# Last feed-forward layer's second product as three products of split parts, with the activations split by GpSimd and the weights split between key tiles

## What is computed

```python
def _L1_xattn_ref(q, k, mask, Wq, bq, Wk, bk, Wv, bv, Wo, bo):
    qh = einsum('bld,dh->blh', q, Wq) + bq
    kh = einsum('bld,dh->blh', k, Wk) + bk
    vh = einsum('blh,hv->blv', kh, Wv) + bv
    scores = where(mask == 0, -10000, einsum('bqh,bkh->bqk', qh, kh))
    return einsum('blh,hv->blv', softmax(scores) @ vh, Wo) + bo

def _L1_ffn_ref(x, W1, b1, phases, w_real, w_imag, W2, b2):   # D_FF = 1024
    hidden = einsum('bsd,df->bsf', x, W1) + b1
    imag = w_imag * sin(phases + hidden * 0.1)
    qphase = cos(phases) * w_real + sin(phases) * w_imag
    act = relu(hidden + qphase * imag * 0.1)
    return einsum('bsf,fd->bsd', act, W2) + b2

x = _layernorm(x + _L1_xattn_ref(x, ctx, mask, ...))
x = _layernorm(x + _L1_ffn_ref(x, ...))
```

## Time and profile before

| | |
|---|---|
| time, median of 3 runs | 3661.45 us (3659.2 to 3665.86) |
| the profiled execution | 3662.63 us, its span 3660.8 us |
| mean granted TensorE clock | 0.976 |
| busy share of the span | PE 93%, PEld 70%, DVE 72%, ACT 61%, POOL 28% |
| phase 3, main part | from 3079 us to the end |

### The profile page before, as it was taken

One profiled execution on the slowest core, in us unless ns is written; L12 is line 12 of the kernel. 1 busy time (PEld: TensorE's weight loads), 2 busy tenths in 40 slices (PEclk: granted clock), 3 DMA queues, 4 the chain that ended last, 5 costly groups with the idle time before them and its releaser, 6 DMA issues.

```text
span 3660.8 us, 61512 instructions
## 1 busy us (share of the span) xinstructions
PE 3401.6 (93%) x21474; PEld 2561.6 (70%) x21474; DVE 2627.9 (72%) x7168; ACT 2226.4 (61%) x4067; POOL 1008.0 (28%) x1560
## 2 busy tenths in 40 slices
PE   4999999999999948999999999999999876999998
PEld 3677777777777636777777777777777655766664
DVE  5588888888888754667777776777777643788876
ACT  3577767776777632455555555555555643677776
POOL 1144434444444431222222222222222210000000
PEclk8999999999999979999999999999999987999999
DMA  6554445545564221444444444444444421011010
GB/s 190 88 92 90 79 83 102 107 75 87 94 104 79 33 87 31 77 82 92 87 86 92 92 89 93 87 90 93 91 87 84 76 38 75 12 35 35 24 35 23
DMA packets 203410, 283.39 MB, mean 77 GB/s; under 512 B 48929, under 2 KB 131874, under 8 KB 194274
## 3 DMA queue, kind: packets, MB, share of 16 engines
q1 hardware_dynamic: 203106, 279.46, 39.0%
HBM read 179.49 MB, written 96.73 MB: 75 GB/s over the span
## 4 chain that ended last, share of the span: by engine, by line
PE 78%; DMA 6%; DVE 6%; ACT 4%; issue 3%; POOL 2%; SPq 1%; PEld 0%; POOLq 0%; PEldq 0%; ACTq 0%; DVEq 0%
PE ps L827 36%; PE ps L1001 10%; PE ps L975 9%; PE ps L1015 7%; PE ps L1199 5%; DMA k_stack<-qk_scratch 5%; PE ps L950 2%; PE ps L979 2%; PE ps L1075 1%; ACT pt L1677 1%; POOL pt L1877 1%; PE ps L1026 1%; PE ps L989 1%; SPq L2002 1%; PE ps L885 1%
## 5 line engine op out<-in xcount | busy, mean ns | idle before, releaser
L1677 ACT ACTIVATE pt<-ps 128x512 f32<-128x512 f32 x1280 | 723.3, 597 | 272.1 <-PE ps L1001 225.6
L1877 POOL TENSOR_SCALAR_AFFINE_SELECT pt<-pt 128x256 f32<-128x256 f32 x1024 | 389.2, 416 | 897.9 <-ACT pt L1677 897.8
L975 PE MATMUL ps<-k_stack,q_stack 96*128 96x512 f32 (+3 forms) x2048 | 587.8, 347 | 34.2 <-DMA k_stack<-qk_scratch 21.9
L1356 DVE CUSTOM_DVE_ANT_0 ps<-ps,future 128x512 f32<-128x512 f32 (+3 forms) x1024 | 482.3, 515 | 101.0 <-PE ps L975 94.7
L1001 PE MATMUL ps<-q_stack,k_stack 100*128 100x512 f32 (+3 forms) x2048 | 532.2, 342 | 14.7 <-ACT pt L1677 10.3
L975 PEld LDWEIGHTS ps<-k_stack,q_stack 96*128 96x128 f32 x2048 | 385.0, 194 | 118.4 <-DMA k_stack<-qk_scratch 26.6
L1349 DVE TENSOR_REDUCE nmax<-ps 128x1 f32<-128x512 f32 (+2 forms) x768 | 359.8, 505 | 120.4 <-PE ps L979 117.2
L1001 PEld LDWEIGHTS ps<-q_stack,k_stack 100*128 100x128 f32 x2048 | 344.8, 192 | 86.9 <-ACT pt L1677 35.5
L1883 POOL TENSOR_TENSOR rs<-rs,mhalf 128x4 f32<-128x4 f32 x96 | 97.1, 1011 | 1057.6 <-DVE rs L1392 1056.2
L1015 PE MATMUL ps<-pt,v_ones 128*32 128x512 f32 (+3 forms) x4096 | 304.9, 438 | 8.0 <-POOL pt L1877 8.0
L1661 ACT ACTIVATE q_stack<-ps 4x512 fp32r<-4x512 f32 x512 | 260.9, 573 | 54.3 <-PE ps L989 51.7
(11 more groups left out here) (276 smaller groups left out, 7969.9 us busy)
## 6 DMA issues: line engine op xcount, KB each, us to landing
qk_scratch<-parts SPq DMA_DIRECT2D x64, 1024.0 KB, 5.7
q_stack<-qk_scratch SPq DMA_DIRECT2D x384, 128.0 KB, 6.2
k_stack<-qk_scratch SPq DMA_DIRECT2D x384, 128.0 KB, 6.7
gate_of<-gate_scratch SPq DMA_DIRECT2D x128, 256.0 KB, 6.3
x_mid<-x_ring SPq DMA_DIRECT2D x32, 512.0 KB, 4.0
x_ring<-x_mid SPq DMA_DIRECT2D x32, 512.0 KB, 5.0
x_ring<-in_x SPq DMA_DIRECT2D x16, 512.0 KB, 3.9
out_dram<-x_ring SPq DMA_DIRECT2D x16, 512.0 KB, 2.9
```

Source lines behind the costliest of these rows:

```text
L975: done = e.matmul(bank(bank_of[piece])[:, at:at + width], a.q[0:96, base + h, t * P:(t + 1) * P], a.k[0:96, base + h, 0:width], start=True ...
L1356: done = e.tensor_tensor_reduce(src, src, future[:, SEQ - width:SEQ], -1.0, 3e38, ALU.add, ALU.min, nmax[:, g % 2, u // 5 * 2 + h, t:t + 1])
L1677: e.activation(dst, src, ACT.Exp).then_inc(exp_up.sem)
L1877: done = e.affine_select(out=blk, in_=blk, compare_op=ALU.is_ge, fill=0.0, base=0, pattern=[[0, 2], [1, P]], channel_multiplier=-1)
```

## The change

- `fd` becomes three fp32r products for each half of the outputs (six matmuls of 512 columns instead of two float32 ones), with the weights `wf2` as high and low parts in phase 3's weight buffer.
- GpSimd gets a piece `fc`: act_h = copy of act in fp32r, then act_l = act - act_h, both 128 x 512. It waits for ACT's `fc` of this block and for PE's `fd` of block i-3. PE's `fd` waits for GpSimd; ACT's `fc` waits for GpSimd's split of block i-3 instead of PE's `fd` of i-3.
- Phase 3's weights are six chunks. Two are split ahead of the key tiles, as they must be, and chunks 2 to 5 behind key tiles 1, 3, 5 and 7; the PE's warming matmuls start after one chunk instead of two. The separate load of w_down is gone.
- The table of phase 3 is new. Orders of one period, from `fa` 0 of item b on (' is item b-1):
  - PE before: fa0 cs fd6' fd7' fa1 fa2 bk' cp fa3 tm cw fd0 fa4 fd1 fa5 fd2 fa6 fd3 fa7 fd4 tc-x1 fd5 tc-ff
  - PE after: fa0 fd5' fd6' fd7' fa1 bk' fa2 cp fa3 tm fd0 fa4 cw fa5 fd1 fa6 fd2 fa7 fd3 tc-x1 fd4 tc-ff cs
  - DVE before: fa0 ce fb0 fa1 ln-ff' fb1 fa2 lm-ff' fa3 fb2 ln-x1 fb3 fa4 lm-x1 fb4 fa5 fb5 fa6 fa7 fb6 fb7 tc-x1 cw tc-ff cs
  - DVE after: fa0 ce fb0 fa1 ln-ff' fb1 fa2 lm-ff' fa3 fb2 ln-x1 fb3 fa4 lm-x1 cw fa5 fb4 fb5 fa6 fa7 fb6 tc-x1 fb7 cs tc-ff
  - ACT after: fa0 ce fb0 bk' fa1 fc0 fa2 fb1 cp fa3 fc1 fb2 lm-ff' fc2 fb3 fa4 cw fa5 fc3 fb4 lm-x1 fc4 fb5 fa6 fa7 fc5 fb6 tc-x1 fc6 fb7 fc7 tc-ff
  - POOL after: fc0 ln-ff' fc1 fc2 ln-x1 fc3 to fc7
- In phase 1's prologue `ab` and `trig` are loaded ahead of x, four[0] of each head moves from DVE to ACT, and the copy into the query stack from ACT to GpSimd, behind its constants.

```diff
-    dict(xqT=CT * 256, xk=CT * 256, xv=CT * 256, xo=CT * 256, w1=CT * FF),
+    dict(xqT=CT * 256, xk=CT * 256, xv=CT * 256, xo=CT * 256, w1=CT * FF, w2=FT * DIM),
...
-    3: (31.45, {
+    3: (32.91, {
...
+        act_h, act_l = (sb(st3, f"act_{part}", [P, DEEP, SEQ], F32R) for part in "hl")
...
-        wf1 = W3.get("w1", CT)
+        wf1, wf2 = W3.get("w1", CT), W3.get("w2", FT)
...
-        W3_READY = n
+        W3_READY = n - len(W3.chunks) + 2
...
-                    e.wait_ge(w_lo.sem, W3_READY - 2)
+                    e.wait_ge(w_lo.sem, W3_READY - 1)
...
                 elif kind == "fd":
                     b, i = key
-                    e.wait_ge(*fc_up[key])
+                    e.wait_ge(*fc_parts[key])
...
                     for c in range(CT):
-                        done = e.matmul(bank(6 + c), wf2[:, i, c * P:(c + 1) * P], act[:, i % DEEP, :], start=i == 0,
-                                        stop=i == FT - 1)
+                        cols = slice(c * P, (c + 1) * P)
+                        done = product(e, bank(6 + c), three(wf2[0][:, i, cols], wf2[1][:, i, cols],
+                                                             act_h[:, i % DEEP, :], act_l[:, i % DEEP, :]),
+                                       start=i == 0, stop=i == FT - 1)
...
-                                e.tensor_scalar(four[:, i, 0, :], trig[:, 0, :], ab[:, 0, h:h + 1], None,
-                                                ALU.mult).then_inc(mine.up())
-                                e.wait_ge(*mine.now)
+                                if h >= 2:
+                                    e.wait_ge(q_lo, h - 1)
+                                e.wait_ge(q_part, h + 1)
...
-                    for w, at, cols, n in chunks[ph]:
+                    for w, at, cols, n in chunks[ph][:2] if ph == 3 else chunks[ph]:
...
+                            if q % 2 and q < 8:
+                                w, at, cols, n = chunks[3][2 + q // 2]
+                                e.wait_ge(w_hi.sem, n + 1)
+                                e.tensor_tensor(w.lo[:, at:at + cols], w_stage3[:, n % STAGES, 0:cols],
+                                                w.hi[:, at:at + cols].bitcast(F32), ALU.subtract).then_inc(w_lo.sem)
...
                             if h >= 2:
                                 e.wait_ge(q_lo, h - 1)
+                                e.wait_ge(q_copy, h - 1)
                             e.activation(fhi[:, i, :], four[:, i, 1, :], ACT.Copy).then_inc(q_fhi)
-                            e.wait_ge(q_fhi, h + 2)
-                            e.activation(att[0].q[0:64, h, :], fhi[0:64, i, :].bitcast(F32), ACT.Copy).then_inc(q_copy)
...
                     if before[0] >= 0:
-                        e.wait_ge(*fd_up[before])
+                        e.wait_ge(*fc_parts[before])
                     e.wait_ge(*fb_add[key])
                     e.activation(act[:, k, :], ang[:, k, :], ACT.Relu, bias=b1_c[:, i:i + 1]).then_inc(fc_up.sem)
...
+                    for h in range(HEADS):
+                        e.wait_ge(q_fhi, h + 2)
+                        e.tensor_copy(att[0].q[0:64, h, :], fhi[0:64, h % 2, :].bitcast(F32)).then_inc(q_copy)
...
+                elif kind == "fc":
+                    b, i = key
+                    k = i % DEEP
+                    before = (b, i - DEEP) if i >= DEEP else (b - 1, (FT - 1) - (FT - 1 - k) % DEEP)
+                    if before[0] >= 0:
+                        e.wait_ge(*fd_up[before])
+                    e.wait_ge(*fc_up[key])
+                    e.tensor_copy(act_h[:, k, :], act[:, k, :]).then_inc(mine.up())
+                    e.wait_ge(*mine.now)
+                    e.tensor_tensor(act_l[:, k, :], act[:, k, :], act_h[:, k, :].bitcast(F32),
+                                    ALU.subtract).then_inc(fc_parts.sem)
...
+            e.dma_start(ab[:, :, :], dram["alpha_beta"]).then_inc(trig_in, 16)
+            e.dma_start(trig[:, :, :], dram["trig"]).then_inc(trig_in, 16)
...
-                        e.dma_start(wf2[:, :, :], dram["w3"][:, W3.cols:].rearrange("p (a b) -> p a b", a=FT)).then_inc(
-                            down_in, 16)
```

More of the change, by code:

```diff
@@ L293 @@
     }),
-    3: (31.45, {
+    3: (32.91, {
         "tensor": {
[L296 to L304, removed]
+            "cw": [-38.588],
+            "tc x1": [-33.614],
+            "cs": [-27.151],
+            "cp": [-10.955],
+            "tm co": [-9.23],
+            "tc ff": [3.566],
+            "fa": [40.979, 48.94, 52.482, 55.475, 60.122, 60.142, 60.162, 61.634],
+            "fd": [59.158, 60.158, 61.235, 64.813, 68.576, 81.727, 81.817, 81.837],
+            "bk 3": [84.663],
         },
         "scalar": {
[11 rows of a table removed]
[11 rows of a table added]
         },
         "vector": {
[L320 to L330, removed]
+            "cw": [-25.459],
+            "tc x1": [-23.476],
+            "cs": [-23.22],
+            "ce": [-21.222],
+            "ln x1": [-4.026],
+            "lm x1": [3.694],
+            "tc ff": [9.733],
+            "fa": [43.552, 47.579, 53.23, 56.308, 66.543, 74.765, 75.126, 75.177],
+            "fb": [47.505, 49.154, 58.326, 64.188, 75.035, 75.055, 75.208, 75.293],
+            "ln ff": [81.556],
+            "lm ff": [87.13],
         },
         "gpsimd": {
-            "ln x1": [-4.648],
-            "ln ff": [82.365],
+            "ln x1": [-21.4],
+            "fc": [27.13, 34.601, 35.155, 46.342, 54.963, 55.239, 59.252, 59.984],
+            "ln ff": [61.42],
         },
         "sync": {
-            "ld 3": [-34.372],
-            "st 3": [85.767],
+            "ld 3": [-51.53],
+            "st 3": [64.89],
         },
@@ L849, in decoder @@
             "keys_up", "keys_tile", "keys_hi", "keys_lo", "bq_up", "bq_parts", "circle_up", "sin_up"))
-        ctx_in3, ctx_parts3, mask_in3, ff_in3, down_in = (mark(n) for n in (
-            "ctx_in3", "ctx_parts3", "mask_in3", "ff_in3", "down_in"))
+        ctx_in3, ctx_parts3, mask_in3, ff_in3 = (mark(n) for n in (
+            "ctx_in3", "ctx_parts3", "mask_in3", "ff_in3"))
         chunks, n = {}, 0
@@ L935, in tensor @@
                 if kind == "prologue" and key[0] == 2:
-                    e.wait_ge(w_lo.sem, W3_READY - len(W3.chunks) - 2)
+                    e.wait_ge(w_lo.sem, W3_READY - 4)
                     warm(bank(7)[:, 0:P], 20)
@@ L1567, in scalar @@
                         e.activation(fhi[:, 2, :], trig[:, 2, :], ACT.Copy).then_inc(q_fhi)
+                        e.activation(four[:, 0, 0, :], trig[:, 0, :], ACT.Copy, scale=ab[:, 0, 0:1]).then_inc(q_part)
                         for h in range(HEADS):
                             i = h % 2
+                            if h + 1 < HEADS:
+                                if h:
+                                    e.wait_ge(q_four, h)
+                                e.activation(four[:, 1 - i, 0, :], trig[:, 0, :], ACT.Copy,
+                                             scale=ab[:, 0, h + 1:h + 2]).then_inc(q_part)
                             e.wait_ge(q_four, h + 1)
@@ L1627, in scalar @@
                                              ACT.Copy).then_inc(keys_hi)
+                            if q % 2 and q < 8:
+                                w, at, cols, m = chunks[3][2 + q // 2]
+                                e.wait_ge(w_in[m % STAGES].sem, 16 * (m // STAGES + 1))
+                                e.activation(w.hi[:, at:at + cols], w_stage3[:, m % STAGES, 0:cols],
+                                             ACT.Copy).then_inc(w_hi.sem)
                         for n in range(2):
@@ L1821, in gpsimd @@
             stops = 0
+            mine = own["gpsimd"]
             for piece in walk["gpsimd"]:
```

10 lines of the change are left out of this document (4 added, 6 removed), and 22 rows, old and new, of the table TABLE.

## The result

The changed kernel takes 3751.16 us (median of 4, 3745.01 to 3755.72) against 3663.65 before; the ratio is 1.0232, with an interval of 1.022 to 1.0245. It is slower, as forecast, but by 87 us where 33 were forecast, and outside the range of 3632 to 3715.

What follows compares the result with a forecast made beforehand. Phase 3 was taken as PE-bound before, then bound by DVE, `cs` and waits for GpSimd. Periods +38, last items -2, phase 1 -5 and phase 3's prologue +2 gave +33: 3694 us, range 3632 to 3715.

Steps and rivals of the forecast that it cites:

- the bound before: Phase 3 before the change: PE-bound, busy 32.96 of 32.96 us at full clock, with DVE next at 26.75.
- the gain of `fd`: PE in phase 3: each `fd` saves 0.35 us, eight save 2.8 per item, leaving PE alone at 30.2.
- the circle of DVE and `cs`: Phase 3's new order: DVE's sequence and PE's `cs` close a loop of 31.9 us, longer than PE's 30.2.
- the lock, with L1545 in it: DVE and GpSimd in phase 3: long instructions exclude each other on the shared port, and one-input L1545 waits too.
- rival 2: Phase 3: only DVE instructions with two inputs wait and L1545 runs through; period 33.7, total 3665; chance 0.12.
- the sum of the waits: DVE's waits for GpSimd's split in phase 3: 4.0 us per item, making the period 35.9 against 32.97.
- the walk: Step through one phase 3 period in the new orders: 31.9 us without GpSimd's waits, 35.9 with them.
- I leave its clock at full: PE in phase 3: idles about 5 us per period in holes below 2 us, with no loss of clock counted.
- the tail, "-2": Last three items: 8 us less for PE, mostly lost to waits, and 1.9 of split behind the last relu: -2.
- The small terms: Prologues: phase 1 and its 14 following heads -5 us, phase 3 +2, and the load of w_down 0.
- the +2: Phase 3's prologue: earlier warming -1.2 us, weight chunks on ACT delaying key tiles +3.2, together +2.
- the term for the 13 periods: Phase 3's 12 periods and the run-up to item 0: 13 times 2.9 us, +38.

Runs made afterwards that it cites:

- small_split: The changed kernel with GpSimd's copy and subtraction cut to 8 columns instead of 512 from the second item on: 3658.85 us, ratio 0.9984.
- tc_ff_first: The changed kernel with PE's `tc ff` one place earlier, ahead of `fd` 4: 3731.49 us, ratio 1.0177.
- under 4: Three clock runs: changed kernel with PE's `tc ff` earlier, 3731.49 us; with `cs` later, 3773.26; with `tc ff` earlier and 8-column splits, 3658.56.
- unused_split: The changed kernel with phase 3's old order and float32 product, GpSimd splitting into parts that nothing reads: 3727.01 us, ratio 1.0173.
- phase1_only: The kernel before with the edits of phase 1's prologue alone: 3662.14 us, ratio 0.9989.
- old_order: The changed kernel with the phase 3 table of the kernel before, GpSimd's split put 0.7 behind its relu's place: 3744.09 us, ratio 1.021.

## Why the prediction was wrong

**Right: the bound before and the gain of `fd`.** In `fd` PEld's starts are 0.23 apart (3289.10, 3289.33, 3289.56) instead of 0.43, so eight `fd` take the 2.8 us less that were worked out. (PE's busy time per period at full clock is 31.4 in small_split and 31.6 in tc_ff_first, 1.4 to 1.6 less than before; ends of matmuls are modelled there, and the starts are the better measure.) In phase 3 only 1.0 of it can be had, because the circle of DVE and `cs` stands at 31.9: measured 32.0 without the split.

**Right: the lock, with L1545 in it.** The copy took 0.61 (0.55), the subtraction 1.30 (1.29). The Trainium skill (SBUF — State Buffer, "SBUF: two separate sides") has the lock for two SBUF inputs or a two-port mode and for the whole instruction; the 1.17 to 1.40 of L1554 in 30 of 30 meetings agree for this one-input instruction too, and rival 2 is out.

**Right in its meetings, somewhat short in their sizes: the sum of the waits.** DVE's rows lengthen per item by 2.15 (L1554), 1.94 (L1556), 0.89 (L1405, `lm`'s) and 0.12 (a softmax instruction), 5.1 in all. They lie where the walk had them. In the period from 3258.5 the copy of block 1 holds `lm`'s L1405 for 0.44 and the subtraction an L1556 for 0.98, 1.4 together (walked 1.35); those of block 3 cost 0.44 and 0.97, 1.4 (walked 1.2); those of 4 and 5 cost 0.78, 0.41 and 0.97, 2.2 (walked 1.8); the splits of 0, 2 and 6 cost nothing, as walked. So 5.1 stands against the 4.45 from which the walk took 0.45 back. Taking the clock's share off, the period would be some 36.6 against the forecast 35.9: the waits cost 4.6, not 4.0.

**The step that failed: "I leave its clock at full".** With half-clock stretches the period is 38.93. They cost 1.6 in seven periods and 3.2 in five, 2.3 on the mean, and the runs of tc_ff_first give 2.3 too. In the period shown above the stretch lies in the chain, between `cs` and `fa` 1. Holes below 2 us were foreseen, and they came (1.6 us at most), but their effect on the clock was put at nothing, without a row for it; this is 13 times 2.3, 30 us of the 57 that were missed; the waits' shortfall is 13 times 0.7, 9, and the tail below is 18. What makes the clock fall stays open, as said under 4.

**The second: the tail, "-2".** It is +15.7. Without the split it is 88.0, as before. I had counted PE's saving and one split's latency but no waits, although DVE meets the split in these items as in the others: from `ln ff` of item 12 on, L1554, L1556 and L1405 together take 12 us more than before, and in unused_split, where no product waits for the split, the tail is 11 longer. The clock of the change's tail is 0.90 against 0.94 before; how much of the 15.7 that is was not separated.

**The small terms.** The first `ln` of phase 1 came 6.2 sooner (forecast 5; the first high part of the weights stands at 41.61 instead of 47.20), which all the runs with this edit share (166.0 to 169.2 against 174.2). Phase 3's first `ln` came 3.9 sooner behind phase 2's last where 2 later was forecast; but phase1_only, without any edit of phase 3, has it 3.5 sooner, so the +2 is neither shown nor refuted. The 6.4 more between the two had no term in the sum; over the runs that stretch, in which no edit lies, takes 2839.8 to 2853.1.

With the term for the 13 periods at 78 instead of 38 and the tail at 16 instead of -2, the sum comes out at 91, against the measured 90.

## What to carry over

Before work is moved to an idle engine, list the DVE instructions that share its port (two SBUF inputs, or the fast one-input rate) and walk the chain with the longest moved instruction added to each: GpSimd, busy for 2 of 33 us in each period before, slowed this kernel by 4.6 us per item without a product waiting for its result. If the work must go there, cut it into short pieces, and look in the chain of waits whether its consumer still has room for the latency that this adds: in one order the pieces took 5 us off the period, in the other they added 3 to 7. When a PE-bound loop becomes bound by a circle through other engines, the clock has to be in the sum, and periods are best compared at the same clock.

## What the runs showed of the hardware beyond that

- GpSimd gives the port back between its instructions: four subtractions of 0.46 hold DVE for at most 0.26, one of 1.30 for up to 0.98. By the Trainium skill (SBUF — State Buffer, "Who interferes with whom") the one that issues first has the pair for its whole instruction; that agrees, and what it says of the issue order does too, since each side waits where it comes second: of the 96 copies from item 0 to 12, 24 that began during an L1556 took 0.8 to 1.1 instead of 0.61, and the 24 L1405 that began during a copy took 0.60 instead of 0.16.
- A DVE instruction of 4 columns (L1405) waits 0.44 us: the width doesn't protect it.
- PE can spend 3.4 to 6.8 us of a 38 us period at 1.2 GHz with no hole above 1.7 us in that period, and in another order (old_order) stay at 2.4 GHz with 14% idle time.
